# A two-layer graph network on one core: more gathers done by matmul, comparison numbers read from PSUM, and a shorter lead for GpSimd

## The reference

```python
# layer 0: an MLP on each edge, summed at its destination
tmp = concatenate([x[dst], x[src], edge_attr_32])        # 48 + 48 + 32 = 128
msg = relu(tmp @ W1 + b1) @ W2 + b2                      # 128 -> 128 -> 48
x = layernorm(x + segment_sum(msg, dst))
# layer 1: a sum and a relu on each edge
m = relu(x[src] + edge_attr_48)
x = layernorm(x + (1 + eps) * x + segment_sum(m, dst))
```

## Time and profile before

| | us |
|---|---|
| three timed runs | 4407.39, 4453.33, 4467.84 |
| their median | 4453.33 |
| the profiled execution | 4415.78 |
| its span, first to last instruction | 4413.9 |
| mean granted TensorE clock of it, as a share of 2.4 GHz | 0.863 |

### The profile page before, as it was taken

The page is one execution under the profiler, slowest core; times in us unless marked ns, Lnnn a source line. Parts: engine busy times, 40 slices in busy tenths (PEclk is TensorE's granted clock), DMA queues, the critical chain, the costliest instruction groups (busy, mean ns, idle before and its releaser), DMA issues.

```text
span 4413.9 us, 56486 instructions
## 1 busy us (share of the span) xinstructions
PE 3796.9 (86%) x21170; PEld 2973.1 (67%) x21170; DVE 2131.5 (48%) x4283; ACT 664.9 (15%) x1275; POOL 2860.8 (65%) x2700
## 2 busy tenths in 40 slices
PE   4678888898999889899997898889689787897988
PEld 2556666676677667677766676668568576675777
DVE  1233333343333334334334576657468565674655
ACT  1212221122122122122221000000000000000111
POOL 6566666666666656656563677767678767676763
PEclk8678998898888888888887898889789998898888
DMA  4122222222222222222221122222122222221221
GB/s 99 28 34 32 33 34 32 32 35 32 34 32 35 32 32 34 32 32 34 35 35 33 41 49 48 46 43 53 39 46 55 45 45 44 43 52 39 50 48 41
DMA packets 407403, 178.33 MB, mean 40 GB/s; under 512 B 279173, under 2 KB 406291, under 8 KB 407027
## 3 DMA queue, kind: packets, MB, share of 16 engines
q0 software_dynamic: 86272, 66.43, 10.8%
q1 hardware_dynamic: 318738, 107.75, 10.7%
q10 hardware_dynamic: 2114, 0.49, 0.1%
HBM read 169.43 MB, written 5.00 MB: 40 GB/s over the span
## 4 chain that ended last, share of the span: by engine, by line
PE 65%; another core or an unknown queue 13%; issue 11%; POOL 5%; DVE 5%; DMA 0%; DVEq 0%; ACT 0%; POOLq 0%; SPq 0%
PE ps_h L830 12%; PE ps_t L830 12%; PE ps_early L830 11%; PE ps_m L740 8%; PE ps_h L791 7%; PE ps_as L732 6%; POOL edge L542 5%; PE ps_t L758 4%; PE ps_nodes L840 2%; PE ps_as L777 2%; DVE picked L1046 1%; DVE edge L957 1%; DVE at_place L1037 1%; DVE acc L971 1%
## 5 line engine op out<-in xcount | busy, mean ns | idle before, releaser
L542 POOL DMA_INDIRECT edge<-x,resid_sb x1438 | 1444.6, 1005 | 884.0 <-issue 405.3
L542 POOL DMA_INDIRECT edge<-x_dram,resid_sb x1258 | 1416.0, 1126 | 621.1 <-issue 381.8
L830 PE MATMUL ps_h<-x_parts,at_place 125*128 125x480 f32 x3080 | 772.7, 401 | 71.6 <-issue 64.1
L830 PE MATMUL ps_t<-x_parts,at_place 125*128 125x480 f32 x3040 | 771.5, 406 | 57.1 <-issue 54.8
L830 PE MATMUL ps_early<-x_parts,at_place 125*128 125x480 f32 x2520 | 706.7, 427 | 94.3 <-DVE edge L957 47.3
L830 PEld LDWEIGHTS ps_h<-x_parts,at_place 125*128 125x128 f32 x3080 | 600.4, 198 | 204.6 <-issue 104.3
L830 PEld LDWEIGHTS ps_t<-x_parts,at_place 125*128 125x128 f32 x3040 | 598.3, 201 | 185.8 <-issue 90.0
L830 PEld LDWEIGHTS ps_early<-x_parts,at_place 125*128 125x128 f32 x2520 | 498.1, 199 | 293.0 <-issue 170.5
L1037 DVE TENSOR_TENSOR at_place<-place_row,places_sb 125x1280 fp32r<-125x1280 f32 x432 | 640.1, 1482 | 1.4 <-DMA place_row<-rows_dram 1.2
L732 PE MATMUL ps_as<-edge,msg 128*48 128x48 f32 x6256 | 367.8, 222 | 219.1 <-issue 173.9
L732 PEld LDWEIGHTS ps_as<-edge,msg 128*48 128x48 f32 x6256 | 300.7, 132 | 330.0 <-issue 261.8
(11 more groups left out here) (63 smaller groups left out, 1769.0 us busy)
## 6 DMA issues: line engine op xcount, KB each, us to landing
e_sb<-e SPq DMA_DIRECT2D x196, 192.0 KB
place_row<-rows_dram SPq DMA_DIRECT2D x432, 62.5 KB
edge<-e SPq DMA_DIRECT2D x196, 128.0 KB
edge<-x,resid_sb POOLq DMA_INDIRECT x1438
edge<-x_dram,resid_sb POOLq DMA_INDIRECT x1258
x_win<-xT SPq DMA_DIRECT2D x391, 9.0 KB
acc<-xT SPq DMA_DIRECT2D x10, 234.4 KB
feats<-x SPq DMA_DIRECT2D x10, 234.4 KB
```

The source lines that it names most:

```text
L542: pool.indirect_dma_start(out=cols, out_offset=None, in_=rows_of, in_offset=bass.IndirectOffsetOnAxis(ap=index, axis=0)).then_inc(done, 16)
L830: last = nc.tensor.matmul(banks[q % len(banks)], lhsT=at_place[:, q % PLACED, c, :], rhs=x1_parts[:, c, part, :], start=(c == 0 and part = ...
```

## The change

The planner's rate for layer 1 goes from 8 to 9 units per group (from 7 to 8 late in the layer), its comparisons may start up to 0.4 steps later. Layer 0 gets one whole pick in each step from 19 to 187. `places_sb` is copied once into a PSUM tile, `ps_places`, which shares a bank with `ps_m`, and `find_places` reads it there. In layer 0 `find_places` moves into `offset_messages`, ahead of the two bias adds of the same step. GpSimd waits for group g - 6 instead of g - 8; the ring stays at 8. It makes 169 and 345 picks.

```diff
@@ plan
-                picks.append((select + 1, math.floor(begun - 1.9), select))
+                picks.append((select + 1, math.floor(begun - 1.5), select))
@@ plan_pairs
-    for s in range(first, last - 2, 4):
-        for begin, end in ((s, s), (s + 1, s + 1), (s + 2, s + 3)):
-            q, each = len(picks), CHUNKS // (end - begin + 1)
-            for step in range(begin, end + 1):
-                units[step] = [(q, (step - begin) * each + c) for c in range(each)]
-            picks.append((2 * (end + 2) + 1, begin - 1, end + 1))
+    for step in range(first, last):
+        units[step] = [(len(picks), c) for c in range(CHUNKS)]
+        picks.append((2 * (step + 2) + 1, step - 1, step + 1))
@@
+LEAD = 6
-PLAN, PRODUCTS = plan([(s, 10 if s < 0 else 8 if s < UNROLL * NORM_ITER else 7) for s in range(-AHEAD, GROUPS)], GROUPS - 1)
+PLAN, PRODUCTS = plan([(s, 10 if s < 0 else 9 if s < UNROLL * NORM_ITER else 8) for s in range(-AHEAD, GROUPS)], GROUPS - 1)
@@ build
-        ps_m = pb("ps_m", [P, 2, TILES, D])
-        ps_iota = ps_m[:, 0, 0, 0:WIN]
+        ps_out = pb("ps_out", [P, 2 * TILES * D + CHUNKS])
+        ps_m = ps_out[:, 0:2 * TILES * D].rearrange("p (g t f) -> p g t f", g=2, t=TILES)
+        ps_iota = ps_out[:, 0:WIN]
+        ps_places = ps_out[0:NP, 2 * TILES * D:]
@@ gathers
-                    wait_for(pool, S[read], g - RING)
+                    wait_for(pool, S[read], g - LEAD)
@@ vector, prologue
+            link(nc.vector.tensor_copy(ps_places, places_sb[:, :]))
@@ offset_messages
                 if pair(p):
                     wait_for(dve, S0["msgp"], pair(p)[-1])
+                for q, (_, find, _) in enumerate(PLAN0):
+                    if find == p + 2:
+                        find_places(S0, q)
                 for g in pair(p):
                     add_b2(S0["msg"], g % UNROLL)
@@ steps0 of VectorE
                 offset_messages(p - 2)
-                for q, (_, find, _) in enumerate(PLAN0):
-                    if find == p:
-                        find_places(S0, q)
@@ find_places
-                                        places_sb[:, :].unsqueeze(2).to_broadcast([NP, CHUNKS, P]), ALU.is_equal).then_inc(S["places"], 1)
+                                        ps_places.unsqueeze(2).to_broadcast([NP, CHUNKS, P]), ALU.is_equal).then_inc(S["places"], 1)
```

## The result

| | before, us | after, us | ratio after / before |
|---|---|---|---|
| first chip, median (lowest to highest) | 4454.84 (4407.39 to 4467.84) | 4554.49 (4544.48 to 4564.75) | 1.0244, 95% interval 1.0165 to 1.0322 |

The changed kernel is slower, by 2.4%, and the whole interval lies above 1. Forecast were 4145 us and a range of 3970 to 4350; the time came out above both, 50 us from what the slow rival gave (4604).

A forecast was written before the change was run, and what follows sets the result against it. GpSimd was taken to have the longer need in both layers, the rest being stalls. Layer 0's -191 us and layer 1's -90 us took 4415.78 to 4135 us; the median was put at 4145 us, range 3970 to 4350.

The forecast's parts named there:

- the slow rival: Both layers: TensorE's stalls have nothing to do with GpSimd, so its excess stays and added picks cost extra; 4604 us, chance 0.10.
- What bounds the kernel: Both layers: GpSimd needs 9.56 us a step and 4.53 a group; 11.87 and 5.11 pass, the rest is stalls.
- Comparison in PSUM: Both layers: gathers beside the comparison no longer stretched, mean 0.97 us in layer 0, 0.99 in layer 1; VectorE costed at nothing.
- the dearer rule: VectorE: the skill's 125 ns access overhead on PSUM against 60 on SBUF, 33 us more for 514 comparisons, off the path.
- More picks: 169 picks in layer 0, 345 in layer 1: TensorE +1.12 us a step and +0.44 a group; fewer gathers for GpSimd.
- Comparison ahead of the bias, six groups ahead: Layer 0's messages come 1.5 us later, under some 4 us of cover; GpSimd's shorter lead ends stalls about 8 us sooner.
- What takes the place of the wait: Both layers: TensorE becomes the longer need, GpSimd pauses about 1.1 us a step, 0.4 a group, and most stalls go.
- TensorE's excess over its need: Time passed beyond TensorE's own need: from 2.95 to 0.70 us a step, from 1.17 to 0.50 a group.
- the picks' own 1.12 us: Layer 0: the added picks raise TensorE's mean need by 1.12 us a step, to 10.04 us.
- The reading under that step: Both layers: TensorE's events and instructions fall behind while GpSimd gathers without a pause, and catch up when it pauses.
- The start level: The forecast times of the changed kernel: 10.74 us a step in layer 0, 4.88 us a group in layer 1.

The follow-up runs named there:

- e5: The kernel before, unchanged, on chip 7 (quick): 3828.72 us, one run.
- e7: The changed kernel with the comparison reading its numbers from SBUF again, on chip 7 (quick): 3915.61 us, ratio 1.0223 to the kernel before.
- e6: The changed kernel, unchanged, on chip 7 (quick): 3845.61 us, ratio 1.0034 to the kernel before.
- e1: The kernel before with the comparison in PSUM and ahead of the bias adds, eight groups ahead, chip 7 (quick): 3503.26 us, ratio 0.9161.
- e3: The kernel of e2 with the changed kernel's 169 picks in layer 0, on chip 7 (quick): 3693.4 us, ratio 0.9653 to the kernel before.
- e15: The changed kernel, unchanged, on chip 11 (stalling): 4608.12 us, ratio 1.0153 to the kernel before.
- e14: The kernel of e2 on chip 11 (stalling): 4659.65 us, ratio 1.0254 to the kernel before.
- e2: The kernel before with the comparison in PSUM and ahead of the bias adds, six groups ahead, chip 7 (quick): 3503.37 us, ratio 0.9159.
- e13: The changed kernel without the gathers of tiles 1 and 2 from group 17 on, chip 11 (stalling): 3863.01 us, one run; kernel before 4550.75.
- e16: The kernel of e1 on chip 13 (stalling): 4682.96 us, ratio 1.0323 to the kernel before.

## Why the prediction was wrong, step by step

**What bounds the kernel.** That GpSimd has the longer need in both layers was right, and on a quick chip it is the whole truth (e5). That the rest of the time is stalls was right for the first chip. How far this depends on the chip no row of one trace could tell.

**Comparison in PSUM.** That a comparison with one input in PSUM leaves the gathers short was right, and the size of the gathers' gain a little small (0.959 and 0.951 us for 0.97 and 0.99). The Trainium skill ("SBUF — State Buffer", Who interferes with whom) says that a VectorE instruction with two SBUF inputs contends with a GpSimd instruction that reads SBUF, and one with a single SBUF input does not; e7 against e6, 1172 and 946 ns, agrees. VectorE's price at nothing was right too: 1483 ns from SBUF (e5) and 1481 from PSUM (e1), so the 33 us of the dearer rule are not there.

**More picks.** 4.4 us of TensorE each was right: 4.42 in layer 0 (e3) and 3.9 in layer 1 (e6 over e3). The added picks were to be half of the cure, by turning GpSimd into the engine that pauses. On the quick chips they are what spends the gain; on a stalling chip they cost nothing (e15 against e14).

**Comparison ahead of the bias, six groups ahead.** The first was costed at nothing, the second as a help in stalls. The place of the comparison was never run by itself. On a quick chip the lead is worth nothing (e1, e2); for the stalls it is open.

**What takes the place of the wait** is the step that failed. I took TensorE's excess over its need to fall from 2.95 to 0.70 us a step and from 1.17 to 0.50 us a group, because GpSimd would pause regularly. It did pause regularly, and the excess fell to 11.92 - 10.04 = 1.88 and stayed at 2113 / 384 - 4.38 = 1.12. In layer 0 that is just the picks' own 1.12 us taken out of the stalls; in layer 1 not even that. The slow rival was said to decide from 1.83 and 0.73 on; both are passed, the first only just. That rival gave 4604 us, and I had put 0.10 on it. That it came within 50 us is luck: it rests on stalls that have nothing to do with GpSimd, which e13 refutes, and it has the excess of layer 0 stay, which fell by 1.07 us.

The reading under that step was half right. That the stalls are tied to GpSimd's gathers was right: e13 takes 57% of them away and the time falls by 745 us at the same work of TensorE. Events do come late, as I had read, but in a stall TensorE's own instructions also come on a beat of 0.70 us, which I had overlooked. The Trainium skill's sentence in the same section, "PE and ACT never wait on anyone", was named with the slow rival; e13 against e15 shows TensorE losing hundreds of us to something that goes with the gathers, though not by which way. Wrong was the second half, that regular short pauses heal. The stall in the profile after comes behind runs of only seven gathers, and e16 has both GpSimd's idle time and the worst ratio of the stalling chips. In the earlier trace rows the pause stood beside the end of the stall; I read the order as a cause, and the rival's own words for it ("a stalled TensorE fills the ring and so makes GpSimd pause") fit as well. What the runs put in its place is a fact and no mechanism yet: on a stalling chip, fewer gathers free TensorE, and the same number of shorter gathers (e16, e14) go with more of the stall. That the rate counts, rather than their number, was argued and not shown; nor do the runs part GpSimd's issuing from the transfers that it starts, or either from the recording of them. The cause of the stalls stays open.

**The start level.** On a quick chip the changed kernel's step is 10.61 us where I had written 10.74, its group 4.49 for 4.88. The first agrees by luck, since the 0.70 us over the need were meant for what is left of the stalls, and there are none on such a chip. And there the kernel before has no stalls to lose either, 10.06 and 4.68, and the ratio is 1.003.

## What to carry to other kernels

When two engines' needs lie within a few per cent, do one thing at a time: freeing the one (comparison in PSUM, 8.4% on quick chips) and loading the other (82 picks, 342 us) cancel, and e2, the first edit without the second, is the version to keep there: 3503 us against 3827 and 3846. On the stalling chips neither version beats the kernel before (1.0254 and 1.0153), so a time from one chip is not enough to choose by.

An instruction that waits long for an event which the trace shows as long past is not explained by what ends beside it. Take the suspected cause away at unchanged work (e13) before building a forecast on it. And count the records of a trace before trusting what it shows of a wait: those of the stalling chips lack nearly a third of the engines' updates.

## What was not expected of the hardware

- The same kernel takes 3823 to 3836 us on four chips and 4455 to 4551 us in four other visits, and they differ in more than speed: one edit gives 0.916 on the one kind and 1.032 on the other. How much of this is the chip, the occasion or the recording is open.
- On the stalling chips ACT and VectorE start many us after the matmuls that they wait for (1265.14 to 1272.33 above, 1532.23 to 1542.91 in the earlier trace rows), while TensorE's matmuls go on for a time and then come on the beat of 0.70 us. On chip 7 ACT follows at once. The same place of a step on chip 7, where ACT starts on the first half of ps_h while the second is still being written:

```profile
1059.21 1.95 PE L790 MATMUL ps_h<-edgeT,w_edge 128*128 128x512 f32 x4
...
1060.34 0.69 ACT L644 ACTIVATE hT<-ps_h,b_sb 128x512 f32<-128x512 f32 x1 [3.32 <-PE ps_h L790]
```

- The stalls need the gathers: with 57% of them left out chip 11 runs at 3863 us and 97% TensorE, close to what chip 7 shows (3791).
